# Expert results of a perceiver kernel collected rank by rank behind the row gathers, and spare rows filled in another stage

## The chip, the cores and the metric

The kernel runs on one core of one Trainium2 chip. The metric is the device time of one execution in microseconds (us), shown as the median of three timed runs. The core has TensorE (PE: matrix products; PEld is its weight load), VectorE (DVE), ScalarE (ACT), GpSimd (POOL) and SyncE (SP); sixteen DMA engines move data between HBM and the on-chip memories SBUF and PSUM. SP, ACT and POOL each issue DMAs on a queue of their own.

## The reference

Two layers of a perceiver in float32, on x of 16 x 64 tokens (1,024 tokens of 256 numbers) and a context of 16 x 1,601 rows of 256. Each layer adds three blocks to x, each on a layer-normalised x:

```
x += cross attention over ctx_1024 (masked)            # layer 0: "x0"
x += latent attention, 16 heads of 16, causal
x += position-routed feed-forward, 8 matrices
x += cross attention over ctx_1024                     # layer 1: "x1"
x += state-space mixer
x += mixture of experts:
      scores = sigmoid(x @ gate_w.T);  4 of 8 groups, then the 8 best of 64 experts
      w = scores of the 8 / their sum * 2.5
      y = sum over the 8 of  w * (silu(x @ Wg) * (x @ Wu)) @ Wd
      + a shared expert
```

The last block is the one that the larger part of the change touches: 8,192 (token, expert) pairs.

## The kernel before

**Cross attention x0.** Eight steps, one for each pair of batches. Step p needs two loads from HBM: ctxT(p), the context by columns (`load_columns`, L202, 3,202 KB), for the scores (L302), and ctxN(p), the same by rows (`load_rows`, L205 and L208, 3,202 KB together), for the products with the probabilities (L327). Both are double-buffered. SP issues ctxT(p+2) once scores(p) are done, and ctxN(p+1) once the products of step p-1 are done; all of it goes through SP's one queue, in program order. TensorE's order in a step is scores(p), products of p-1, transposes of p, and the output of p-1. After step 1's loads SP runs `x0_second` (L2195): the sixteen small weight loads of the latent attention (L129) and then eight DMAs (L2199) from HBM to HBM that fill y_rows from row 8,192 on with rows of x. These are the spare rows: tiles 64 to 127 of y_rows, which may be read without having been written in this execution. Then come ctxT(4), ctxN(3), ctxT(5) and so on. ACT waits for the fill (`s_spare`, L2078) before the expert tiles, over 600 us later. The latent attention's own SP block issues only one DMA, `WF.loads`, the 2 MB of feed-forward weights. Cross attention x1 is the same code with other weights; its `x1_second` issues the mixer's weights (about 3.3 MB) in the place of the fill.

**Experts: the routing.** DVE finds for each token its eight experts, and for each pair a slot, which is a row number in y_rows; `slots8` holds a token's eight slots in descending order (MAX8), so rank k = 7 is the smallest slot and k = 0 the largest. One-hot tiles (`of_tile`, `in_tile`, L1892, L1893) and products on TensorE (L1740, L1744) turn this into a list of tokens by slot (`idxt`, L1901).

**Experts: the tiles.** Slots are worked off in tiles of 128 rows, in rounds of six (RING = 6): 6 rounds of tiles that have their own weights, then 7 rounds in which two tiles' worth of weights serve three tiles; 78 tiles in all. For tile n POOL gathers 128 rows of x (L2086), TensorE turns and multiplies them (L1979, L1998, L2016), DVE copies and multiplies (L2037, L2045), ACT evaluates silu (L2062), copies the result (L2067) and stores it in y_rows (L2077). DVE hands POOL the index column of tile n + 5 in step n (L2029), and tile n's store is issued in step n + 7. After the last gather POOL waits until all rounds are stored.

**Experts: the collection.** A block of its own behind the tiles. For j = 0 to 7 (128 tokens each) and k = 0 to 7, POOL gathers the 128 rows of y_rows that hold the tokens' result of rank k (L2128, 64 indirect DMAs of 128 KB). Meanwhile DVE works out the weights (L2140 to L2159, 30 instructions), waits for the eight gathers of a j and adds them (L2171, 64 instructions), and ACT stores each j (L2135).

Of the kernel before, what the change touches and what calls it, by code (L numbers as in the profile page):

```python
# [40 lines left out]
def perceiver(nc, a, out):  # L41
    with ExitStack() as ctx:
        def sb(name, shape, dt=F32, own=ctx, side="left"):
            return own.enter_context(nc.sbuf_tensor(name, shape, dt, side=side))
        def sem(name, own=ctx):
            return own.enter_context(nc.semaphore(name))
# [687 lines left out]
        def latent_and_ffn(w, prep, x1, sem):  # L734
# [11 lines left out]
            def latent_attention():  # L746
# [882 lines left out]
        def experts(w):  # L1629
# [24 lines left out]
            w8 = own("w8", [P, NT, 8])  # L1654
            pick = own("pick", [P, NT, E])
            in_tile = own("in_tile", [P, 2, 4, P, 2], BF16)
            RING = 6
            LEAST, MOST = 2, 21
            LEAST2, MOST2 = 1, E // 4
# [39 lines left out]
            s_im = sem("moe_index_product")  # L1699
            with nc.Block(no_gpsimd_drain=True) as block:  # L1700
# [4 lines left out]
                def _(pe):  # L1705
# [79 lines left out]
                def _(dve):  # L1785
# [98 lines left out]
                    nc.vector.tensor_copy(place[:], sloti[:, 1:3, :, :])  # L1884
                    dve.drain()
                    for j in range(NT):
                        u = j % 2
# [5 lines left out]
                        nc.vector.tensor_tensor(in_tile[:, u], bc(count2[:], 1, 4), pairs_of(place[:, 1, j, :], P), ALU.is_equal).then_inc(s_oh, 1)  # L1893
                    dve.wait_ge(s_im, NT)
# [32 lines left out]
            s_ys = [sem(f"tile_stored{m}") for m in range(RING)]  # L1927
            GU, DOWN, AHEAD = 3, 6, 5
# [13 lines left out]
            def run(eng, step, lag):  # L1942
                for n in range(LEAST * RING):
                    step(n, n % RING, n // RING, None, lambda k, n=n: n >= k)
# [9 lines left out]
                with eng.Fori(LEAST, first) as g:  # L1954
                    whole(g)
# [16 lines left out]
            with nc.Block(no_gpsimd_drain=True) as block:  # L1972
# [54 lines left out]
                def _(dve):  # L2027
# [21 lines left out]
                    run(dve, step, GU)  # L2049
                @block.scalar  # L2050
                def _(act):
# [27 lines left out]
                    run(act, step, DOWN + 1)  # L2079
                @block.gpsimd  # L2080
                def _(pool):
                    def step(n, m, g, q, live):
# [5 lines left out]
                                                     ).then_inc(s_ga[m], 16)  # L2088
                    run(pool, step, 0)
                    rounds = whole_rounds(pool) + shared_rounds(pool)  # L2090
# [3 lines left out]
                def _(sp):  # L2094
# [12 lines left out]
                    for g in range(LEAST):  # L2107
# [3 lines left out]
                    with sp.Fori(LEAST, first) as g:  # L2111
                        whole(g)
# [4 lines left out]
            yg = own("yg", [P, NT, 8 * D])  # L2117
            s_yg = [sem(f"moe_collected{r}") for r in range(NT)]
            s_yl = [sem(f"moe_collected_last_{x}") for x in ("middle", "one")]
            s_ya = sem("moe_result_added")  # L2120
            def collected(j, k):
                return s_yg[j] if j < NT - 1 or k < 4 else s_yl[k // 7]
            with nc.Block(no_gpsimd_drain=True) as block:  # L2123
                @block.gpsimd
                def _(pool):
                    for j in range(NT):
                        for k in range(8):
                            nc.gpsimd.indirect_dma_start(out=yg[:, j, k * D:(k + 1) * D], out_offset=None, in_=y_rows[0:MOST_TILES * P, :],  # L2128
                                                         in_offset=bass.IndirectOffsetOnAxis(ap=sloti[:, 0, j, k:k + 1], axis=0)
                                                         ).then_inc(collected(j, k), 16)  # L2130
                @block.scalar
                def _(act):
                    for j in range(NT):
                        act.wait_ge(s_ya, j + 1)
                        act.dma_start(out.rearrange("(j b) s d -> j (b s) d", b=2)[j], xt[:, j, :]).then_inc(s_out, 16)  # L2135
                    act.wait_ge(s_out, 16 * NT)
                @block.vector
                def _(dve):
                    def choice_weights():
                        nc.vector.tensor_tensor(cwt[:], sg[:], rep[:], ALU.mult)  # L2140
                        dve.drain()
                        nc.vector.tensor_reduce(tot[:], cwt[:], AX, ALU.add)
                        dve.drain()
                        nc.vector.tensor_scalar(tot[:], tot[:], 1e-20, None, ALU.add)
                        dve.drain()
                        nc.vector.reciprocal(tot[:], tot[:])
                        dve.drain()
                        nc.vector.tensor_scalar(tot[:], tot[:], 2.5, None, ALU.mult)
                        dve.drain()
                        nc.vector.tensor_tensor(cwt[:], cwt[:], bc(tot[:], 2, E), ALU.mult)  # L2150
                        dve.drain()
                    def weight_third(i):
                        k, third = i // 3, i % 3
                        if third == 0:
# [7 lines left out]
                    for i in range(24):  # L2162
                        weight_third(i)
# [173 lines left out]
```

## Time and profile before

| | us |
|---|---|
| median of three runs | 927.86 |
| the three runs | 921.66, 927.86, 929.37 |
| the profiled execution | 924.3 |
| its span in the trace | 922.5 |

The page of the profile gives busy time by engine: PE 690.4 us (75% of the span), PEld 473.8, DVE 447.2, ACT 243.6, POOL 249.8. Its strip of 40 slices shows where the bound lies: PE is busy in nearly all of the first 36 slices, the DMA engines are full in the two cross attentions and in the expert tiles, and in the last four slices PE does nothing while POOL and DVE work. The mean granted clock of TensorE is 0.845 of full speed (2.4 GHz). A line of a timeline is: start, duration, engine, source line, operation, output and inputs, number of merged instructions, and in brackets the engine's idle time before it and what ended it. SPq and ACTq are DMA issues; the duration of a merged row reaches from the first to the last.

### The profile page before, as it was taken

What the parts mean: (1) busy time and instruction counts of PE and PEld (TensorE: products, weight loads), DVE (VectorE), ACT (ScalarE), POOL (GpSimd) and SP (SyncE); (2) the same over time, 40 slices, a digit from 0 to 9 for tenths busy, and PEclk for the clock granted to TensorE, in tenths of its full rate; (3) what the DMA queues carried; (4) which work ended last, traced back from release to release, by engine and by line L of the source; (5) the groups of instructions that cost most, each with busy time, mean ns of one, the idle gap of its engine ahead of it and who ended that gap; (6) DMA issues with size and microseconds to landing.
All of it is one profiled execution on the core that took longest, in us unless ns stands there. A gap on an engine that the chain in (4) does not pass through costs nothing. (4 is left out here: it accounts for less than half of the span.)

```text
span 922.5 us, 18970 instructions
## 1 busy us (share of the span) xinstructions
PE 690.4 (75%) x6637; PEld 473.8 (51%) x6637; DVE 447.2 (48%) x1114; ACT 243.6 (26%) x471; POOL 249.8 (27%) x289
## 2 busy tenths in 40 slices
PE   6798389896867699998899979796649899990000
PEld 4355155644645355555654468685448777770000
DVE  4333023357756452232436649858834334437534
ACT  1122021166445121211223644203412223330000
POOL 1011000020134120000000436512235445526775
PEclk9899699988968599999979965579779999995555
DMA  8999999420028969999117942001049999972343
GB/s 344 380 402 330 355 404 410 159 91 1 2 58 316 322 246 334 405 411 392 72 35 163 213 114 74 4 2 47 1 132 334 331 304 300 310 259 88 116 115 105
DMA packets 70888, 195.62 MB, mean 212 GB/s; under 512 B 11832, under 2 KB 43552, under 8 KB 65824
## 3 DMA queue, kind: packets, MB, share of 16 engines
q1 hardware_dynamic: 41248, 155.31, 47.6%
q10 hardware_dynamic: 22752, 20.72, 6.8%
q0 software_dynamic: 6816, 18.62, 6.8%
q8 instruction: 46, 0.75, 0.3%
q14 instruction: 26, 0.21, 0.1%
HBM read 181.05 MB, written 21.95 MB: 220 GB/s over the span
## 5 line engine op out<-in xcount | busy, mean ns | idle before, releaser
L2086 POOL DMA_INDIRECT moe_xg<-xn_rows,moe_idx x78 | 73.9, 948 | 83.4 <-DVE moe_idx L2029 72.3
L2128 POOL DMA_INDIRECT moe_yg<-y_rows,moe_sloti x64 | 64.0, 1000 | 37.2 <-issue 19.2
L302 PE MATMUL ps<-x0ctxT,x0qcur 128*64 128x512 f32 (+1 forms) x256 | 51.9, 562 | 22.8 <-DMA x0ctxT<-ctx_T 18.4
L1472 POOL TENSOR_TENSOR ss_dec<-ss_dec,ss_cT 128x256 f32<-128x256 f32 x48 | 39.7, 860 | 91.4 <-ACT ss_dec L1427 51.3
L2045 DVE TENSOR_TENSOR moe_hidT<-moe_silu,ps 128x128 f32<-128x128 f32 (+1 forms) x64 | 20.3, 317 | 80.5 <-ACT moe_silu L2062 59.6
L1285 PE MATMUL ps<-xnT,w_win 128*128 128x512 f32 x128 | 59.0, 620 | 0.0
L327 PE MATMUL ps<-x0ctxN,x0pT 128*64 128x256 f32 (+1 forms) x416 | 46.6, 381 | 7.4 <-issue 5.2
L327 PE MATMUL ps<-x1ctxN,x1pT 128*64 128x256 f32 (+1 forms) x416 | 46.6, 380 | 7.4 <-issue 5.2
L1317 PE MATMUL ps<-ss_dec 64*64 64x32 f32 (+2 forms) x1792 | 46.1, 256 | 6.1 <-issue 4.5
L91 POOL TENSOR_TENSOR rstd<-vare,neghalf 128x2 f32<-128x2 f32 (+1 forms) x10 | 11.2, 1125 | 139.5 <-DVE vare L87 139.5
L2062 ACT ACTIVATE moe_silu<-ps 128x128 f32<-128x128 f32 (+1 forms) x64 | 19.2, 300 | 109.0 <-issue 72.2
L302 PEld LDWEIGHTS ps<-x0ctxT,x0qcur 128*64 128x64 f32 x256 | 18.7, 150 | 57.1 <-issue 40.1
L302 PE MATMUL ps<-x1ctxT,x1qcur 128*64 128x512 f32 (+1 forms) x256 | 46.9, 520 | 1.0 <-POOL x1qcur L568 1.0
L2171 DVE SCALAR_TENSOR_TENSOR xt<-moe_yg,moe_w,xt 128x256 f32<-128x256 f32 x64 | 31.1, 486 | 33.8 <-DMA moe_yg<-y_rows,moe_sloti 29.1
L1317 PEld LDWEIGHTS ps<-ss_dec 64*64 64x64 f32 (+2 forms) x1792 | 39.7, 172 | 12.0 <-issue 7.1
L327 PEld LDWEIGHTS ps<-x0ctxN,x0pT 128*64 128x64 f32 (+1 forms) x416 | 32.2, 137 | 20.3 <-issue 9.3
L327 PEld LDWEIGHTS ps<-x1ctxN,x1pT 128*64 128x64 f32 (+1 forms) x416 | 32.3, 137 | 19.8 <-issue 9.0
L1998 PE MATMUL ps<-moe_xgT,e_shared_gate_up_weights 128*128 128x192 f32 x224 | 41.7, 330 | 0.1
L1285 PEld LDWEIGHTS ps<-xnT,w_win 128*128 128x128 f32 x128 | 25.1, 199 | 30.7 <-issue 30.3
L1979 PE MATMUL ps<-ident,moe_xg 128*128 128x128 f32 x156 | 32.4, 291 | 10.4 <-DMA moe_xg<-xn_rows,moe_idx 10.3
L1545 DVE COPY_PREDICATED ss_gm<-w_c_lvl,ps 128x128 f32<-128x128 int32 (+1 forms) x80 | 30.7, 384 | 18.6 <-ACT ss_gm L1441 13.1
L1998 PE MATMUL ps<-moe_xgT,moe_gate_up_weights 128*128 128x128 f32 x288 | 39.3, 281 | 0.0
(387 smaller groups left out, 1384.6 us busy)
## 6 DMA issues: line engine op xcount, KB each, us to landing
x0ctxT<-ctx_T SPq DMA_DIRECT2D x8, 3202.0 KB, 25.4
x1ctxT<-ctx_T SPq DMA_DIRECT2D x8, 3202.0 KB, 13.6
x0ctxN<-ctx SPq DMA_DIRECT2D x8, 3072.0 KB
x1ctxN<-ctx SPq DMA_DIRECT2D x8, 3072.0 KB
y_rows<-moe_ysb ACTq DMA_DIRECT2D x78, 128.0 KB
moe_gate_up_weights<-moe_gate_up SPq DMA_DIRECT2D x36, 256.0 KB, 4.5
e_shared_gate_up_weights<-moe_gate_up SPq DMA_DIRECT2D x28, 256.0 KB, 4.9
ss_dec<-seg_rows SPq DMA_DIRECT2D x8, 768.0 KB, 17.0
```

Source lines behind the costliest of these rows:

```text
L302: mm = pe.matmul(ps[64 * b:64 * b + 64, n, 0:k1 - k0], qcur[:, u, h, 64 * b:64 * b + 64], ctxT[:, u, b, h, k0:k1], start=h == 0, stop=h == ...
L327: mm = pe.matmul(ps[64 * b:64 * b + 64, 6, 0:D], pT[0:k, u, c, 64 * b:64 * b + 64], ctxN[0:k, u, b, c, :], start=c == 0, stop=c == NC_ - 1)
L1285: mm = pe.matmul(ps[:, 2 * slot[i] + n, :], win[:, h, m * P:(m + 1) * P], xnT[:, h, n * 512:(n + 1) * 512], start=h == 0, stop=h == DH - 1)
L1317: return pe.matmul(dst, f, g, start=True, stop=True)
L1472: e.tensor_tensor(f, f, g, ALU.mult).then_inc(s, 1)
L1545: ins = nc.vector.copy_predicated(old, bc(mask, 1, 4), new)
L1979: mm = pe.transpose(ps[:, TURNED[m % 3], h * P:(h + 1) * P], xg[:, m, h * P:(h + 1) * P], ident[:])
L1998: mm = pe.matmul(ps[:, PRODUCT[place % 3], x * w:(x + 1) * w], weights[:, h, x * FE:(x + 1) * FE], xgT[:, h, col:col + w], start=h == 0, s ...
L2045: nc.vector.tensor_tensor(hidT[:, col:col + w], silu[:, col:col + w], ps[:, PRODUCT[place % 3], w:2 * w], ALU.mult).then_inc(s_hh, tiles)
L2086: nc.gpsimd.indirect_dma_start(out=xg[:, m, :], out_offset=None, in_=xn_rows, in_offset=bass.IndirectOffsetOnAxis(ap=idx[:, m:m + 1], axis ...
L2128: nc.gpsimd.indirect_dma_start(out=yg[:, j, k * D:(k + 1) * D], out_offset=None, in_=y_rows[0:MOST_TILES * P, :], in_offset=bass.IndirectO ...
L2171: ins = nc.vector.scalar_tensor_tensor(xt[:, j, :], y[:, k, :], w8[:, j, k:k + 1], xt[:, j, :], ALU.mult, ALU.add)
```

## The change

- The eight fill DMAs of spare rows move from `x0_second` (SP, middle of cross attention x0) to the latent attention's SP block, behind `WF.loads`.
- The block of the collection is gone. POOL collects in the block of the tiles, directly behind its last row gather, and by rank: k = 7 first, k = 0 last, for each k all eight j. Ahead of a rank it loads a number of rounds from SBUF (`needed`), and waits until that many rounds are stored, with six waits on a register's value.
- The routing works out `needed`: for each rank the largest slot over all tokens, divided by 768, plus one. That is one reduction over j on DVE, a transpose on PE, a second reduction, a one-row product and five instructions on eight numbers.
- DVE works out the weights directly behind its last tile, in the same block, and adds by rank; for k = 0 it waits for each j alone. The 64 additions and 64 gathers are as many as before. The buffer `yg` (64 KB per partition) is now held beside the tiles' buffers.
- The written-out rounds stay two (WRITTEN); the least numbers of rounds rise from 2 and 1 to 3 and 2, which the data's 6 and 7 exceed.

```diff
@@ latent attention, sync
                         issue(sp, WF.loads)
+                        for r in range(SPARE):
+                            t0, t1 = T * 8 // P + r * NT, min(T * 8 // P + r * NT + NT, MOST_TILES)
+                            sp.dma_start(y_rows[t0 * P:t1 * P, :], a["x"].rearrange("b s d -> (b s) d")[0:(t1 - t0) * P, :]).then_inc(s_spare, 16)
@@ routing, tensor
+                    pe.wait_ge(s_lt, 1)
+                    pe.transpose(ps[0:8, 2, 0:P], latest[:], ident[:]).then_inc(s_lr, 1)
                     for j in range(NT):
+                        if j == 4:
+                            pe.wait_ge(s_lt, 2)
+                            pe.matmul(ps[0:1, 2, P:P + 8], latest_row[:, 0:1], ident[0:8, 0:8], start=True, stop=True).then_inc(s_lr, 1)
@@ routing, vector
+                    nc.vector.tensor_reduce(latest[:], slots8[:].rearrange("p j k -> p k j"), AX, ALU.max).then_inc(s_lt, 1)
                     dve.drain()
                     for j in range(NT):
+                        if j == 2:
+                            dve.wait_ge(s_lr, 1)
+                            nc.vector.tensor_reduce(latest_row[:], ps[0:8, 2, 0:P], AX, ALU.max).then_inc(s_lt, 1)
...
+                    dve.wait_ge(s_lr, 2)
+                    nc.vector.tensor_scalar(latest_int[:], ps[0:1, 2, P:P + 8], -1.0, None, ALU.add)
+                    dve.drain()
+                    nc.vector.tensor_scalar(latest_int[:], latest_int[:], 7, None, ALU.arith_shift_right)
+                    dve.drain()
+                    nc.vector.tensor_scalar(latest_int[:], latest_int[:], 171, None, ALU.mult)
+                    dve.drain()
+                    nc.vector.tensor_scalar(latest_int[:], latest_int[:], 10, None, ALU.arith_shift_right)
+                    dve.drain()
+                    nc.vector.tensor_scalar(needed[:], latest_int[:], 1, None, ALU.add)
                     dve.wait_ge(s_im, NT)
@@ tiles, vector
                     run(dve, step, GU)
...
+                    choice_weights()
+                    for i in range(24):
+                        weight_third(i)
+                    for k in reversed(range(8)):
+                        if k:
+                            dve.wait_ge(s_yg[k], 16 * NT)
+                        for j in range(NT):
+                            if k == 0:
+                                dve.wait_ge(s_yl[j], 16)
+                            ins = nc.vector.scalar_tensor_tensor(xt[:, j, :], yg[:, k, j, :], w8[:, j, k:k + 1], xt[:, j, :], ALU.mult, ALU.add)
+                            if k == 0:
+                                ins.then_inc(s_ya, 1)
+                        dve.drain()
@@ tiles, gpsimd
+                    def collect(k):
+                        rounds = pool.value_load(needed[0:1, k:k + 1], min_val=1, max_val=MOST + MOST2)
+                        stored = nc.gpsimd.to_reg(rounds * 16)
+                        pool.wait_ge(s_rows, 16)
+                        for m in range(RING):
+                            pool.wait_ge(s_ys[m], stored)
+                        for j in range(NT):
+                            nc.gpsimd.indirect_dma_start(out=yg[:, k, j, :], out_offset=None, in_=y_rows[0:MOST_TILES * P, :],
+                                                         in_offset=bass.IndirectOffsetOnAxis(ap=sloti[:, 0, j, k:k + 1], axis=0)
+                                                         ).then_inc(s_yg[k] if k else s_yl[j], 16)
                     run(pool, step, 0)
+                    for k in reversed(range(8)):
+                        collect(k)
                     rounds = whole_rounds(pool) + shared_rounds(pool)
@@ behind the tiles
-            with nc.Block(no_gpsimd_drain=True) as block:
-                @block.gpsimd
-                def _(pool):
-                    for j in range(NT):
-                        for k in range(8):
-                            nc.gpsimd.indirect_dma_start(out=yg[:, j, k * D:(k + 1) * D], out_offset=None, in_=y_rows[0:MOST_TILES * P, :],
...
@@ cross attention x0, sync
-        def x0_second(sp):
-            issue(sp, loads_la)
-            for r in range(SPARE):
-                t0, t1 = T * 8 // P + r * NT, min(T * 8 // P + r * NT + NT, MOST_TILES)
-                sp.dma_start(y_rows[t0 * P:t1 * P, :], a["x"].rearrange("b s d -> (b s) d")[0:(t1 - t0) * P, :]).then_inc(s_spare, 16)
-        cross_attention("x0", w_x0, True, bufs0, x0_first, x0_second, prep)
+        cross_attention("x0", w_x0, True, bufs0, x0_first, lambda sp: issue(sp, loads_la), prep)
```

## Rows read from the trace of the kernel before

**Rows 1.** The page: span, and the chain that ended last, by line.

```profile
span 922.5 us, 18970 instructions
...
POOL moe_yg L2128 7%; DMA moe_yg<-y_rows,moe_sloti 0%; DVE xt L2171 0%; DVEq L2172 0%; PEldq L2123 0%
```

**Rows 2.** Timeline of POOL, end of the tiles and the collection.

```profile
815.29 0.94 POOL L2086 DMA_INDIRECT moe_xg<-xn_rows,moe_idx  x1 [0.86 <-DVE moe_idx L2029]
834.25 0.94 POOL L2128 DMA_INDIRECT moe_yg<-y_rows,moe_sloti  x1 [18.02 <-PEq L2123]
...
916.46 0.95 POOL L2128 DMA_INDIRECT moe_yg<-y_rows,moe_sloti  x1 [0.31 <-issue]
```

**Rows 3.** Timeline of ACT: stores of tile 71 and of the last two tiles.

```profile
826.22 0.35 ACTq L2077 DMA_DIRECT2D y_rows<-moe_ysb  x1
...
829.75 1.92 ACTq L2077 DMA_DIRECT2D y_rows<-moe_ysb  x2
```

**Rows 4.** Timeline of DVE: last tile, first weight instruction, first additions.

```profile
827.88 0.35 DVE L2045 TENSOR_TENSOR moe_hidT<-moe_silu,ps 128x192 f32<-128x192 f32 x1 [1.25 <-ACT moe_silu L2062]
833.59 0.69 DVE L2140 TENSOR_TENSOR moe_cwt<-moe_sg,moe_rep 128x512 f32<-128x512 f32 x1 [5.36 <-PEq L1972]
...
855.46 5.02 DVE L2171 SCALAR_TENSOR_TENSOR xt<-moe_yg,moe_w,xt 128x256 f32<-128x256 f32 x9
```

**Rows 5.** Timeline of SP's queue in cross attention x0.

```profile
56.13 0.37 SPq L129 DMA_DIRECT2D w_wdq<-L_attn_W_DQ  x1
...
70.20 0.42 SPq L129 DMA_DIRECT2D w_kn<-L_attn_k_norm_w  x1
70.66 5.05 SPq L2199 DMA_DIRECT2D y_rows<-x  x8
76.11 0.41 SPq L202 DMA_DIRECT2D x0ctxT<-ctx_T  x1
```

**Rows 6.** DMAs of line L2199, from issue to landing.

```profile
DMA to landing us min/median/max: 6.1/14.7/23.5
```

**Rows 7.** Timeline of PE in x0: scores(3), (4), (7), products of steps 6 and 7.

```profile
75.59 5.60 PE L302 MATMUL ps<-x0ctxT,x0qcur 128*64 128x512 f32 x32
...
106.80 7.94 PE L302 MATMUL ps<-x0ctxT,x0qcur 128*64 128x512 f32 x32 [16.59 <-DMA x0ctxT<-ctx_T]
...
158.46 5.60 PE L302 MATMUL ps<-x0ctxT,x0qcur 128*64 128x512 f32 x32
165.83 5.83 PE L327 MATMUL ps<-x0ctxN,x0pT 128*64 128x256 f32 x52 [1.77 <-issue]
...
175.67 5.84 PE L327 MATMUL ps<-x0ctxN,x0pT 128*64 128x256 f32 x52 [0.60 <-DVE xt L436]
```

**Rows 8.** Stretches: PE, PEld, DVE, ACT, POOL busy (instructions); clock, DMA share, GB/s.

```profile
71.00:98.00 27.00, 18.88 (x134) 11.43 (x130) 7.09 (x15) 4.57 (x8) 0.62 (x2) 0.93 0.97 324
98.00:106.00 8.00, 0.00 (x0) 0.00 (x0) 0.00 (x0) 0.00 (x0) 0.00 (x0) 0.50 1.00 403
106.00:168.00 62.00, 53.92 (x361) 30.83 (x363) 18.24 (x56) 10.96 (x17) 0.80 (x2) 0.96 1.02 401
...
200.00:244.00 44.00, 33.39 (x445) 21.36 (x443) 31.29 (x50) 24.54 (x38) 2.17 (x3) 0.88 0.01 1
```

**Rows 9.** Timeline of PE in x1: scores(3), (4) and (5).

```profile
365.28 5.61 PE L302 MATMUL ps<-x1ctxT,x1qcur 128*64 128x512 f32 x32
...
379.92 5.60 PE L302 MATMUL ps<-x1ctxT,x1qcur 128*64 128x512 f32 x32
...
396.62 5.61 PE L302 MATMUL ps<-x1ctxT,x1qcur 128*64 128x512 f32 x32
```

**Rows 10.** Timeline of DVE: a small reduction, the wait behind the one-hots, a round's turn.

```profile
654.86 0.28 DVE L1867 TENSOR_REDUCE moe_owner<-moe_below 128x2 f32<-128x128 f32 x1
...
677.12 0.29 DVE L1896 COPY moe_home<-ps 128x128 f32<-128x128 f32 x1 [2.76 <-PE ps L1744]
...
705.63 0.15 DVE L2029 TENSOR_SCALAR moe_idx<-moe_idxt 128x1 int32 x1 [1.47 <-issue]
```

More of the change, by code:

```diff
@@ L1654, in experts @@
             w8 = own("w8", [P, NT, 8])
+            yg = own("yg", [P, 8, NT, D])
+            latest = own("latest", [P, 8])
+            latest_row = own("latest_of_choice", [8, 1])
+            latest_int = own("latest_int", [1, 8], I32)
+            needed = own("rounds_needed", [1, 8], I32)
             pick = own("pick", [P, NT, E])
@@ L1927, in experts @@
             s_ys = [sem(f"tile_stored{m}") for m in range(RING)]
+            s_yg = [None] + [sem(f"moe_choice_collected{k}") for k in range(1, 8)]
+            s_yl = [sem(f"moe_last_choice_collected{j}") for j in range(NT)]
+            s_ya = sem("moe_result_added")
             GU, DOWN, AHEAD = 3, 6, 5
@@ L1942, in run @@
             def run(eng, step, lag):
-                for n in range(LEAST * RING):
+                for n in range(WRITTEN * RING):
                     step(n, n % RING, n // RING, None, lambda k, n=n: n >= k)
@@ L1953, in shared @@
                         step(g * RING + m, m, g, q, lambda k: True)
-                with eng.Fori(LEAST, first) as g:
+                with eng.Fori(WRITTEN, first) as g:
                     whole(g)
@@ L2079, in _ @@
                     run(act, step, DOWN + 1)
+                    for j in range(NT):
+                        act.wait_ge(s_ya, j + 1)
+                        act.dma_start(out.rearrange("(j b) s d -> j (b s) d", b=2)[j], xt[:, j, :]).then_inc(s_out, 16)
+                    act.wait_ge(s_out, 16 * NT)
                 @block.gpsimd
@@ L2106, in shared @@
                             load(0 if g is None else g * RING + m, etab[0:1, 1, ds(q * 4 + x, 1)], wgu2[:, x], s_wl2[x])
-                    for g in range(LEAST):
+                    for g in range(WRITTEN):
                         whole(g)
@@ L2110, in _ @@
                     second = shared_rounds(sp)
-                    with sp.Fori(LEAST, first) as g:
+                    with sp.Fori(WRITTEN, first) as g:
                         whole(g)
@@ L2116, in experts @@
             rings.close()
[L2117 to L2122, printed above, removed]
-            with nc.Block(no_gpsimd_drain=True) as block:
-                @block.gpsimd
-                def _(pool):
-                    for j in range(NT):
-                        for k in range(8):
-                            nc.gpsimd.indirect_dma_start(out=yg[:, j, k * D:(k + 1) * D], out_offset=None, in_=y_rows[0:MOST_TILES * P, :],
[L2129 to L2154, printed above, removed]
-                            nc.vector.tensor_tensor(pick[:], slot1[:], bc(slots8[:, :, k], 2, E), ALU.is_equal)
-                        elif third == 1:
-                            nc.vector.tensor_tensor(pick[:], pick[:], cwt[:], ALU.mult)
-                        else:
-                            nc.vector.tensor_reduce(w8[:, :, k], pick[:], AX, ALU.add)
-                        dve.drain()
-                    choice_weights()
-                    for i in range(24):
-                        weight_third(i)
-                    for j in range(NT):
-                        y = yg[:, j, :].rearrange("p (k d) -> p k d", k=8)
-                        for k in range(8):
-                            if k == 0:
-                                dve.wait_ge(s_yg[j], 16 * (8 if j < NT - 1 else 4))
-                            if j == NT - 1 and k in (4, 7):
-                                dve.wait_ge(s_yl[k // 7], 16 * (3 if k == 4 else 1))
-                            ins = nc.vector.scalar_tensor_tensor(xt[:, j, :], y[:, k, :], w8[:, j, k:k + 1], xt[:, j, :], ALU.mult, ALU.add)
-                            dve.drain()
-                        ins.then_inc(s_ya, 1)
```

30 lines of the change are left out of this document (28 added, 2 removed).

## The prediction

> **What bounds the kernel now.** I read the page first. The chain that ended last is POOL's own: the 64 gathers of the collection and nothing else [rows 1]. The timeline of POOL shows why: the last row gather starts at 815.29, then POOL idles 18.02 us for the end of the tiles' block, and the 64 gathers run from 834.25 to 916.46, one each (916.46 - 834.25)/63 = 1.305 us [rows 2]. In these 82 us PE is idle and DVE keeps up. So the end of the kernel is POOL's time: what starts the 64 gathers earlier shortens the kernel one for one. ACT's timeline places the last stores: tile 71 at 826.22, tiles 76 and 77 at about 829.75 and 831.3 [rows 3].
>
> The second place is cross attention x0, which the page's strip shows with full DMAs. The timeline of SP's queue has the small latent weights from 56.13, the eight fill DMAs at 70.66, and only behind them ctxT(4) at 76.11 [rows 5]. The timeline of PE has scores(3) at 75.59 and scores(4) at 106.80, after 16.59 us of waiting for ctxT(4), and then taking 7.94 us instead of 5.60 [rows 7]. So the fill is on the path of x0, not beside it.
>
> **Part 1: the fill leaves x0.** The fill writes tiles 64 to 127, 64 x 128 KB = 8.39 MB. Its last landing is 23.5 us after an issue at about 75.1, so at 98.6 [rows 5, 6]: 28 us of the DMA engines, which move 324 GB/s from 71 to 98 [rows 8]. Behind it nine context loads of 3.28 MB wait in one queue: ctxT(4), ctxN(3), ctxT(5), ctxN(4), ctxT(6), ctxN(5), ctxT(7), ctxN(6), ctxN(7). At the 401 GB/s of the stretch 106 to 168 [rows 8] each takes 8.2 us, together 73.6: 98.6 + 73.6 = 172.2, and the products of step 7 start at 175.67 [rows 7]. Without the fill the same chain starts at 71.5 (SP is free at 70.6, the small latent loads are still in the engines [rows 5]) and ends at 71.5 + 73.6 = 145.1.
>
> PE has a pace of its own. In x1, where the mixer's 3.3 MB stand in the place of the fill, scores(3) and (4) start at 365.28 and 379.92, 14.64 us apart, with no wait [rows 9]. Then x0 would have scores(4) at 75.59 + 14.6 = 90.2 instead of 106.80, and scores(7) at 90.2 + 3 x 14.6 = 134.0. From scores(7) to the products of step 7 it is 17.21 us, of which 1.77 are waiting [rows 7], so 15.4: 149.4. I checked each load against its use: ctxT(4) lands at 80 (used at 90.2), ctxN(3) 88 (95.6), ctxT(5) 96 (104.8), ctxN(4) 104 (110.2), ctxN(5) 120 (124.8), ctxN(6) 137 (139.4), ctxN(7) 145 (149.4). The margin at ctxN(6) is 2.5 us, thin but there. The step gains 175.67 - 149.4 = **26.2 us**. The lower bound is x1's course: there scores(5) follows scores(4) after 16.70 [rows 9], a pace that the loads set. If x0 fell into that too, only scores(4)'s wait goes: 31.21 - 14.64 = 16.6, and 18.73 - 16.70 = 2.0 for the clock (scores(5) start at 106.80 + 18.73 in the trace), 18.6 in all. I take 26.2, because the x0 chain would start 4.1 us ahead of scores(3), while x1's loads wait behind the mixer's weights.
>
> The clock, told by rows: PE's granted clock is 0.93 from 71 to 98, with PE busy for 18.9 of 27 us, and 0.50 (1.2 GHz) from 98 to 106, where PE does nothing [rows 8]; scores(4) start at that lower level, hence their 7.94 us [rows 7]. That goes with the stall and is inside the 26.2.
>
> **Where the fill goes.** The latent attention starts its block near 190.8 - 26; the fill then lies under it for some 28 us behind 2 MB of weights, 37 us together. From 200 to 244 the DMAs move 1 GB/s [rows 8], and the next loads on this queue come at about 270 - 26. ACT's wait for the fill is 500 us later. So it costs nothing; if fetches of instructions, which pass through the same engines (a queue of their own on the page), got stuck behind it, I allow 2 us in the range.
>
> **Part 2: the collection moves up.** Which rounds a rank needs depends on data, so I worked the slots out from the reference's own routing on its inputs: 36 own tiles and 28 shared sets, 6 and 7 rounds, as many weight loads as the trace has. The rounds needed are 7, 10, 10, 12, 12, 13, 13, 13 for k = 7 to 0. POOL could start at 815.29 + 0.94 + 0.30 = 816.5 instead of 834.25: **-17.7 us** [rows 2]. Do the waits cost? Ranks 7, 6 and 5 need round 10, tile 59, whose store is issued before 807. Rank 4 needs round 12, tile 71, issued at 826.22 [rows 3] and landed by about 830; POOL arrives there after 24 gathers, at 816.5 + 24 x 1.305 = 847.8. Rank 2 needs round 13, landed by 834; POOL arrives at 868.7. No wait is ever open, with 17 us to spare, so later stores are covered too.
>
> New on POOL is, per rank, a load of a number from SBUF, a multiplication and seven waits. Before has no such thing between two gathers. The nearest row is DVE's turn from the written-out rounds to the loop, 1.47 us with two such loads [rows 10], so at most 0.7 per load; the lower bound is 0, since the row gathers have two waits and register work ahead of each and still the 0.30 us gap of gathers without any. I take 0.5 each, 8 x 0.5 = **+4.0**, bounds 0 to 8. The Trainium skill, "DMA: Bandwidth & Descriptors", Latency and other measured facts, gives a load of this kind a floor of about 600 ns. By it the term would be an estimated 4.8.
>
> DVE: the weights start behind its last tile, at 828.2 instead of 833.59, and take as long as before, 855.46 - 833.59 = 21.9 [rows 4], to 850.1. By then POOL has 25 gathers out; the additions go at 5.02/9 = 0.56 us [rows 4] against POOL's 1.305, so the backlog is gone by about 865, 30 us before the end. Behind the last gather lie one addition and one store, as before. The gathers from 816 to 831 share the DMAs with the last stores; a tile delayed by a few us hits nobody, as the waits have 17 us.
>
> **Part 3: the routing.** The first reduction (128x64, like 0.28 us [rows 10]) stands ahead of the one-hots on DVE's path: +0.3. The second, the transpose and the small product fall into waits for ACT. The five small instructions, some 0.25 us each with their drains, 1.25, lie in DVE's 2.76 us wait for PE [rows 10]. Without that cover they would cost the 1.25. I take **+0.4**.
>
> **Sum.** 924.3 - 26.2 - 17.7 + 4.0 + 0.4 = 884.8 for an execution like the profiled one. The median of the runs is 3.6 above it; 884.8 + 3.6 = 888.4, so **888 us**.
>
> **Rivals.**
> *x0 goes by its loads.* Gain of part 1 is 18.6 rather than 26.2, time 896. For it: x1's pace of 16.70 and the thin margin at ctxN(6). Against it: the margins above. A rule leads to the same place: at a lower rate the nine loads are late. At 358 GB/s each is 9.2 us, the chain ends at 71.5 + 82.5 = 154, the gain is some 21 and the time 893. The Trainium skill, "DMA: Bandwidth & Descriptors", Where 436 GB/s comes from, puts the limit of HBM loads at about 358 GB/s per core. By that rule this rival would be the forecast; the trace disagrees, with 401 GB/s over 62 us.
> *The collection gains nothing.* If POOL in fact sits until the last store (its waits or its index column tie it to the end), the time is 924.3 - 26.2 + 0.4 + 3.6 = 902. The rounds worked out speak against it.
> *x0 gains nothing*: something else, SP's small loads say, holds ctxT(4). Then 884.8 + 26.2 + 3.6 = 915. Against it: from 71 to 98.6 the queue holds the fill ahead of ctxT(4).
> *The other side: the fill slows the latent attention.* Its 37 us of full DMAs would have to hold up fetches of instructions by more than 26.2 + 17.7 - 4.4 = 39.5 us before the kernel gets no faster, and by 49 for 1% slower. x0 itself ran at PE's full pace under full DMAs, so I hold it to be unlikely.
>
> **How the numbers follow.** Forecast 0.66, x0 by its loads 0.20, collection without gain 0.05, x0 without gain 0.04, fill in the way 0.05 (of it 0.02 slower, 0.01 same, 0.02 still faster). Low end: no load costs and no offset to the median, 888.4 - 4.0 - 3.6 = 881, and 1 or 2 less in x0: 879. High end: the first rival, 896, with 2 us more for loads on POOL: 898. Of the first two cases nearly all lies inside, some 0.8 in all. A measurement of this kernel can tell about 1% from no change (the three runs span 0.8%). Faster by over 1% (under 918.6): 0.66 + 0.20 + 0.05 + 0.04 + 0.02 = 0.97, of which I move 0.01 to same for what I have not seen: 0.96, 0.02, 0.02.
>
> **What the profile after would show.** PE's scores(4) near 90 without a wait for ctxT, scores 14.6 apart and products of step 7 near 149; if they are 16.4 apart, the first rival. A DMA strip with full slices in the latent attention, none of its engines slower. POOL's 64 gathers behind the last row gather, the first within 1.5 us of its end, with no gap above 1 us. A gap of several us ahead of rank 4 or 2 would prove the rounds wrong. DVE's additions waiting for POOL from about the 40th on. The prediction fails if a gap per rank is above 1 us or if the load chain sags below 380 GB/s.

## The result

Medians over several executions, each kernel beside runs of the kernel before on the same chip. One execution of e5 below, at 888.20 us, is over 1.5% slower than the fastest of its kernel and is left out of its median and range.

| | before | after |
|---|---|---|
| median, us | 924.76 | 886.5 |
| lowest and highest, us | 914.96 to 929.37 | 880.23 to 889.74 |
| ratio after/before, 95% interval | | 0.9612 [0.9501, 0.9723] |
| the profiled execution, us | 924.3 | 880.23 |
| its span, us | 922.5 | 878.3 |
| its mean granted clock | 0.845 | 0.86 |

The forecast was 888 us. The kernel became 3.9% faster, and the median is 1.5 us from the forecast. The two spans differ by 44.2 us, where the terms of the sum add up to 39.5. They are followed in order of time.

**Cross attention x0.** The timeline of SP's queue in the kernel after answers to [rows 5], with the fill in its new place behind the weight w_wf (start, duration, engine and line):

```profile
70.51 0.42 SPq L129 DMA_DIRECT2D w_kn<-L_attn_k_norm_w  x1
71.33 0.40 SPq L202 DMA_DIRECT2D x0ctxT<-ctx_T  x1
...
166.36 0.38 SPq L129 DMA_DIRECT2D w_wf<-L_ffn_WT  x1
166.78 6.38 SPq L780 DMA_DIRECT2D y_rows<-x  x8
...
238.18 0.38 SPq L129 DMA_DIRECT2D w_x_wq<-L_xattn_Wq  x1
```

ctxT(4) is issued at 71.33 instead of 76.11. The timeline of PE answers to [rows 7]: scores(3), (4), (5) and (7), then the products of steps 6 and 7.

```profile
75.03 5.61 PE L302 MATMUL ps<-x0ctxT,x0qcur 128*64 128x512 f32 x32
...
89.59 5.60 PE L302 MATMUL ps<-x0ctxT,x0qcur 128*64 128x512 f32 x32
...
104.14 5.61 PE L302 MATMUL ps<-x0ctxT,x0qcur 128*64 128x512 f32 x32
...
133.93 5.60 PE L302 MATMUL ps<-x0ctxT,x0qcur 128*64 128x512 f32 x32
141.35 5.83 PE L327 MATMUL ps<-x0ctxN,x0pT 128*64 128x256 f32 x52 [1.82 <-issue]
...
151.19 5.83 PE L327 MATMUL ps<-x0ctxN,x0pT 128*64 128x256 f32 x52 [0.60 <-DVE xt L436]
```

Nothing waits ahead of scores(4), and scores follow each other after 14.6 us up to the sixth; the seventh comes 15.2 us later, since the products of step 5 waited 0.46 us. The products of step 7 start 175.67 - 151.19 = 24.5 us earlier. The windows answer to [rows 8]: the full clock (1.00, 2.4 GHz) where PE had stood still at 0.50, and one stretch in the latent attention that now has DMA work under it. The first row is the start of the chain of context loads.

```profile
71.00:73.00 2.00, 1.91 (x16) 1.26 (x12) 0.70 (x3) 0.56 (x1) 0.00 (x0) 1.00 0.48 61
71.00:98.00 27.00, 26.66 (x190) 15.15 (x188) 9.23 (x18) 4.79 (x9) 0.80 (x2) 1.00 0.97 380
98.00:106.00 8.00, 7.83 (x55) 4.94 (x53) 2.47 (x6) 2.93 (x5) 0.00 (x0) 1.00 1.01 404
...
166.30:238.20 71.90, 52.70 (x760) 36.27 (x761) 53.55 (x100) 42.04 (x69) 12.47 (x13) 0.94 0.43 147
```

The loads ctxT(4) and ctxT(7), from issue (71.33 and 109.94) to landing:

```profile
DMA to landing us min/median/max: 12.0/12.0/12.0
...
DMA to landing us min/median/max: 22.2/22.2/22.2
```

So ctxT(4) landed at 83.3 and ctxT(7) at 132.1. The same view gives 99.5 for ctxT(5) and 115.7 for ctxT(6).

The latent attention of the kernel before, from the issue of w_wf to that of x1's first weight, in its windows:

```profile
190.80:269.90 79.10, 60.09 (x760) 40.13 (x760) 53.54 (x100) 42.50 (x69) 12.46 (x13) 0.83 0.09 28
```

The same 760 matmuls, DVE busy for as long to 0.01 us, and yet 7.2 us less, at a granted clock of 0.94 instead of 0.83. No step of the prediction had this.

**Routing.** From DVE's MAX8 to the first row gather it takes 22.46 us instead of 21.67, 0.8 more. In DVE's timeline the five new small instructions lie ahead of the copy that waited for PE in [rows 10]; it still waits, 1.76 instead of 2.76:

```profile
643.72 0.14 DVE L1915 TENSOR_SCALAR moe_latest_int<-ps 1x8 int32<-1x8 f32 x1
644.64 0.16 DVE L1923 TENSOR_SCALAR moe_rounds_needed<-moe_latest_int 1x8 int32<-1x8 int32 x1
646.56 0.29 DVE L1926 COPY moe_home<-ps 128x128 f32<-128x128 f32 x1 [1.76 <-PE ps L1760]
```

**The collection.** The timeline of POOL answers to [rows 2]. The rank of the first eight gathers is k = 7, the one at 796.75 is the first of k = 6.

```profile
785.18 0.95 POOL L2158 DMA_INDIRECT moe_xg<-xn_rows,moe_idx  x1 [0.70 <-DVE moe_idx L2062]
786.73 0.95 POOL L2168 DMA_INDIRECT moe_yg<-y_rows,moe_sloti  x1 [0.60 <-DMA y_rows<-moe_ysb]
787.98 0.95 POOL L2168 DMA_INDIRECT moe_yg<-y_rows,moe_sloti  x1 [0.30 <-issue]
...
796.75 0.95 POOL L2168 DMA_INDIRECT moe_yg<-y_rows,moe_sloti  x1 [0.30 <-issue]
...
842.68 1.12 POOL L2168 DMA_INDIRECT moe_yg<-y_rows,moe_sloti  x1 [0.30 <-issue]
844.10 1.67 POOL L2168 DMA_INDIRECT moe_yg<-y_rows,moe_sloti  x1 [0.30 <-issue]
846.08 0.95 POOL L2168 DMA_INDIRECT moe_yg<-y_rows,moe_sloti  x1 [0.30 <-issue]
...
871.77 0.97 POOL L2168 DMA_INDIRECT moe_yg<-y_rows,moe_sloti  x1 [0.30 <-issue]
```

The first gather starts 1.55 us behind the start of the last row gather, instead of 18.96. Between ranks the gap is the usual 0.30 us. But the pace is (871.77 - 786.73)/63 = 1.350 us where before had 1.305, and the reason stands in the second column: some gathers take 1.12 or 1.67 us instead of 0.95. DVE's timeline at that time (compare [rows 4]):

```profile
820.09 9.91 DVE L2114 SCALAR_TENSOR_TENSOR xt<-moe_yg,moe_w,xt 128x256 f32<-128x256 f32 x24
...
841.70 3.26 DVE L2114 SCALAR_TENSOR_TENSOR xt<-moe_yg,moe_w,xt 128x256 f32<-128x256 f32 x8 [7.74 <-DMA moe_yg<-y_rows,moe_sloti]
852.64 3.25 DVE L2114 SCALAR_TENSOR_TENSOR xt<-moe_yg,moe_w,xt 128x256 f32<-128x256 f32 x8 [7.68 <-DMA moe_yg<-y_rows,moe_sloti]
```

The eight additions of a rank run one behind another from 841.70 to 844.96, and the two long gathers lie under them. The kernel before drained DVE behind each addition, that is, let it end before the next was issued; the change drains once per rank.

The account, from the two profiles:

| stretch | before | after | difference | forecast |
|---|---|---|---|---|
| start to the products of x0's step 7 | 175.67 | 151.19 | -24.5 | -26.2 |
| latent attention, w_wf to x_wq | 79.07 | 71.82 | -7.2 | 0 |
| routing, MAX8 to first row gather | 21.67 | 22.46 | +0.8 | +0.4 |
| last row gather's end to the end | 106.27 | 92.17 | -14.1 | -17.7 + 4.0 |

The other stages add up to +0.8: the feed-forward stretch up to x1's first scores -0.7, x1 with the mixer 0.0, the routing's head +1.1, the tiles +0.4. All together: -44.2. Within the last row, -17.4 is the earlier start (18.96 to 1.55), +2.8 the slower pace, and +0.5 lies behind the start of the last gather.

### The profile page after: what moved, and what is told of

Read it like the earlier page. It is cut to its first block and busy times, and to the rows that moved or that the text cites. A ratio compares the mean times of both kernels' runs of the same rounds, so it can differ in the third digit from the quotient of the medians.

```text
span 878.3 us, 18973 instructions
## 1 busy us (share of the span) xinstructions
PE 683.1 (78%) x6640; PEld 472.3 (54%) x6640; DVE 443.2 (50%) x1121; ACT 243.8 (28%) x471; POOL 253.5 (29%) x289
## 5 line engine op out<-in xcount | busy, mean ns | idle before, releaser
L2168 POOL DMA_INDIRECT moe_yg<-y_rows,moe_sloti x64 | 66.8, 1044 | 19.8 <-issue 18.3
L302 PE MATMUL ps<-x0ctxT,x0qcur 128*64 128x512 f32 (+1 forms) x256 | 46.5, 516 | 6.6 <-issue 5.8
L2114 DVE SCALAR_TENSOR_TENSOR xt<-moe_yg,moe_w,xt 128x256 f32<-128x256 f32 x64 | 26.5, 480 | 29.6 <-DMA moe_yg<-y_rows,moe_sloti 29.3
```

The lines of the kernel that those rows point to most:

```text
L302: mm = pe.matmul(ps[64 * b:64 * b + 64, n, 0:k1 - k0], qcur[:, u, h, 64 * b:64 * b + 64], ctxT[:, u, b, h, k0:k1], start=h == 0, stop=h == ...
L2114: ins = nc.vector.scalar_tensor_tensor(xt[:, j, :], yg[:, k, j, :], w8[:, j, k:k + 1], xt[:, j, :], ALU.mult, ALU.add)
L2168: nc.gpsimd.indirect_dma_start(out=yg[:, k, j, :], out_offset=None, in_=y_rows[0:MOST_TILES * P, :], in_offset=bass.IndirectOffsetOnAxis(a ...
```

## The experiments

Each number with brackets behind it is the ratio to the kernel before, with its 95% interval; a range in parentheses is the lowest and highest execution. e3, e8, e10 and e11 fill 16 spare tiles instead of 64; the other spare rows stay unwritten, which the data of this case never read. All the others compute everything. The measure for the collection is the time from the last row gather's end to the end of the span, "the tail stretch": 106.27 us before, 92.17 after.

**Two halves.** e1 is the kernel before with only the fill moved; e2 is the changed kernel with the fill back in x0.

```diff
 e1:                     issue(sp, WF.loads)
+                        for r in range(SPARE):
+                            ... sp.dma_start(y_rows[...], ...).then_inc(s_spare, 16)
...
 x0_second:
-            for r in range(SPARE):
-                ... sp.dma_start(y_rows[...], ...).then_inc(s_spare, 16)
```

> The kernel before with only the eight fill DMAs moved to the latent attention. Theory: the move is worth the 24.5 us by which the products of step 7 came earlier in the changed kernel (175.67 to 151.19), so a time of 0.973 to 0.975 of before, and the products of step 7 at 150 to 152. Rival 1 (the fill only changes its place): the latent attention gives part of it back, ratio above 0.985. Rival 2 (x0 goes by its loads): step 7 at about 157, ratio 0.98.

> The changed kernel with the fill put back into cross attention x0, so that only the collection and the routing differ from before. Theory: from the end of the last row gather to the end of the span 93 us instead of before's 106.3, ratio 0.985 to 0.988 of before (11 to 14 us). Rival: the gathers start early but the tiles' own last rounds are slowed and the end moves by less than 5 us, ratio above 0.995.

e1: 895.24 us (893.53 to 901.73), 0.9681 [0.9612, 0.9751], against 926.84 before. Products of step 7 start at 151.18, as in the changed kernel; the tail stretch is 105.21. e2: 909.65 us (905.91 to 914.94), 0.982 [0.9747, 0.9892]. Products at 176.57, tail stretch 91.0, 2 us less than the 93 expected. Its POOL timeline:

```profile
816.36 0.95 POOL L2155 DMA_INDIRECT moe_xg<-xn_rows,moe_idx  x1 [0.87 <-DVE moe_idx L2059]
817.91 0.95 POOL L2165 DMA_INDIRECT moe_yg<-y_rows,moe_sloti  x1 [0.60 <-DMA y_rows<-moe_ysb]
```

By the medians the fill is worth 31.6 us and the collection 17.2. Together that is 48.8, where the change brought 38.3 in its own measurement and 38.8 in that of e0 below. In the traces the parts do add up: x0 gives 24.5 in e1, which is just what it gives after, and the tail stretch 15.3 in e2 and 14.1 after. What e1 has beyond its 24.5 lies in part in the latent attention, 74.45 us instead of 79.07, where no engine's instructions differ and only the fill's DMAs are new; that is taken up below.

**Is it the rounds that free the collection?** e4 lets every rank wait for all 13 rounds:

```diff
-                        rounds = pool.value_load(needed[0:1, k:k + 1], min_val=1, max_val=MOST + MOST2)
+                        rounds = whole_rounds(pool) + shared_rounds(pool)
                         stored = nc.gpsimd.to_reg(rounds * 16)
```

> The changed kernel, but every rank waits until all 13 rounds are stored, as if the rounds by rank were not known. Theory: the first gather of results then starts when the last store has landed, 17 us behind the last row gather instead of 0.6, and the whole of it reaches the end: 16 to 17 us slower than the changed kernel, near 0.98 of before. Rival: the gain came from the missing block boundary and not from the early start; then it is within 4 us of the changed kernel.

902.18 us (898.05 to 905.3), 0.9723 [0.9655, 0.979]. Its POOL timeline:

```profile
793.61 0.95 POOL L2158 DMA_INDIRECT moe_xg<-xn_rows,moe_idx  x1 [1.01 <-DVE moe_idx L2062]
811.66 0.95 POOL L2168 DMA_INDIRECT moe_yg<-y_rows,moe_sloti  x1 [17.11 <-DMA y_rows<-moe_ysb]
```

The 18 us are back, and the tail stretch is 108.14. By the medians it is 16 us slower than the changed kernel's 886.5 (18 than e0's 884.35), as expected. The last row gather's start and the first gather of results are 18.05 us apart here, 18.96 before. But e1 and e8, which keep the block of its own, have 18.01 and 18.03, so that the collection stands in the tiles' block is worth nothing that the traces show: 0.9 us against one profile, none against two. The gain comes from ranks that ask for early rounds. This is also the prediction's rival "the collection gains nothing", built as a kernel: it was priced at 902.

**What do the number and the seven waits per rank cost?** e6 has the rounds of this data as constants, so neither load nor multiplication:

```diff
-                        rounds = pool.value_load(needed[0:1, k:k + 1], min_val=1, max_val=MOST + MOST2)
-                        stored = nc.gpsimd.to_reg(rounds * 16)
+                        stored = (13, 13, 13, 12, 12, 10, 10, 7)[k] * 16
```

> The changed kernel with the rounds by rank written in as constants (7, 10, 10, 12, 12, 13, 13, 13), so no load and no multiplication per rank on POOL, the waits stay. Theory: the load is hidden behind the gather ahead of it (the gap between ranks is 0.30 us, that within a rank too), so pace and time are those of the changed kernel, the first gap perhaps 0.3 shorter. Rival, the prediction's term: 0.5 us a rank, 4 us less.

e0 is the changed kernel again, beside it on the same chip:

> The changed kernel once more, unchanged, to stand beside the others of this row on the same chip, and for a second profile. Expected: 0.955 to 0.965 of before; collection and cross attention x0 within 0.5 us of the first profile; the latent attention anywhere from 72 to 80 us, with the granted clock from 0.94 to 0.82 to match.

e6: 880.21 us (875.11 to 882.06), 0.9521 [0.9473, 0.957]. e0: 884.35 us (880.59 to 887.37), 0.9572 [0.9521, 0.9623]. The intervals overlap, so the trace must tell. In e6 the first gather follows the last row gather by 1.25 us instead of 1.55, the pace is 1.332 against e0's 1.323, and the tail stretch 90.45 against 90.15. The load costs 0.3 us once and nothing at the other seven ranks.

e0 also shows how far one profile can be trusted. Its x0 and its routing are those of the first profile (products of step 7 at 151.30, routing 22.46), but its pace is 1.323 instead of 1.350 and its tail stretch 90.15 instead of 92.17. That is 2.0 us, where at most 0.5 was expected. The same kernel thus gained 14.1 us in the tail stretch in one execution and 16.1 in the other.

**What makes the gathers slower?** e5 puts the drain back behind each addition; e9 leaves the additions as they are and starts them only when the last gather is in.

```diff
 e5:                         ins = nc.vector.scalar_tensor_tensor(xt[:, j, :], yg[:, k, j, :], ...)
-                        dve.drain()
+                            dve.drain()
 e9:                         weight_third(i)
+                    dve.wait_ge(s_yl[NT - 1], 16)
                     for k in reversed(range(8)):
```

> The changed kernel with a drain behind each of the 64 additions, as before had them, instead of one behind each eight. In the changed kernel the 64 gathers go at 1.350 us each, before at 1.305, and gathers of 1.67 us lie beside DVE's runs of eight undrained additions. Theory: the runs of additions slow POOL; with drains the pace is 1.30 to 1.31 and the end 2 to 3 us earlier than in the changed kernel, none of the gathers behind rank 4 above 1.3 us. Rival 1: the pace comes from the order by rank; it stays at 1.34 to 1.35. Rival 2: it comes from the loads and waits per rank; the same.

> The changed kernel, but DVE starts its 64 additions only when the last gather has landed, so that none of them lies beside a gather; the weights still do. Theory: every gather behind the weights' end (from about the 28th on) takes 0.94 to 0.96 us with a gap of 0.30, a pace of 1.25, and the whole 64 average 1.28 or less; the end comes later by the additions' 26 us less what they overlapped. Rival: some other agent slows POOL; then gathers of 1.1 us and more stay.

e5: 880.59 us (874.88 to 882.24), 0.9535 [0.9491, 0.958]; pace 1.299, tail stretch 89.07. POOL and DVE at the place where the changed kernel has 1.12 and 1.67:

```profile
842.74 0.95 POOL L2168 DMA_INDIRECT moe_yg<-y_rows,moe_sloti  x1 [0.30 <-issue]
843.99 0.95 POOL L2168 DMA_INDIRECT moe_yg<-y_rows,moe_sloti  x1 [0.30 <-issue]
...
841.81 4.45 DVE L2114 SCALAR_TENSOR_TENSOR xt<-moe_yg,moe_w,xt 128x256 f32<-128x256 f32 x8 [3.52 <-DMA moe_yg<-y_rows,moe_sloti]
```

e9, in a single execution (901.84 us, since the additions now stand behind everything):

```profile
842.67 0.94 POOL L2169 DMA_INDIRECT moe_yg<-y_rows,moe_sloti  x1 [0.30 <-issue]
...
870.41 26.56 DVE L2115 SCALAR_TENSOR_TENSOR xt<-moe_yg,moe_w,xt 128x256 f32<-128x256 f32 x64 [50.60 <-DMA moe_yg<-y_rows,moe_sloti]
```

With DVE idle, every gather from the 26th on takes 0.94 or 0.95 us, and the pace over all is 1.278, since gathers under the weights still reach 1.34 (1.47 in e3). So the work of DVE lengthens POOL's gathers, and dense additions do it more: over 64 gathers POOL is busy for

```profile
L2168 POOL DMA_INDIRECT moe_yg<-y_rows,moe_sloti x64 | 66.8, 1044 | 19.8 <-issue 18.3
```

in the changed kernel (line, engine, operation, count, busy and mean ns, idle), and in e5 for

```profile
L2168 POOL DMA_INDIRECT moe_yg<-y_rows,moe_sloti x64 | 63.8, 997 | 19.8 <-issue 18.3 <-DMA y_rows<-moe_ysb 1.5
```

with the same 19.8 of gaps. The size differs between executions: e0 has no gather above 1.28 us beside the additions and 65.2 us in all. But the five undrained profiles whose ranks start early have a pace of 1.323 to 1.350, the four drained ones (e5, e10, e11, e12) 1.297 to 1.307, and the kernel before, drained too, 1.305.

The Trainium skill, "SBUF — State Buffer", Who interferes with whom, says that a DVE instruction with two inputs in SBUF contends with a GpSimd instruction that reads SBUF. The additions have two such inputs (moe_yg and xt), and the gather reads its indices from SBUF; the traces agree with it, at 1.12 to 1.67 us against 0.95. The same section of the Trainium skill infers that such an instruction does not hold up GpSimd's writing of DMA descriptors; if that is part of the gather's time, these traces speak against it. Which of the gather's accesses collides was not separated.

**Does the drained kernel win as a whole?** e12 is e5 again, e10 is e5 with a quarter of the fill, e3 is the changed kernel with it:

```diff
-                        for r in range(SPARE):
+                        for r in range(2):
...
-                    act.wait_ge(s_spare, SPARE * 16)
+                    act.wait_ge(s_spare, 2 * 16)
...
-    in_=y_rows[0:MOST_TILES * P, :]
+    in_=y_rows[0:80 * P, :]
```

> The changed kernel with a drain behind each addition once more, as the partner of the kernel with the quarter fill, on one chip. Theory A and B both: latent attention 72 to 76; 0.950 to 0.957 of before; pace of the gathers 1.30.

> The drained kernel with the fill of 16 tiles instead of 64 in the latent attention. In ten profiles so far the latent attention took 71.8 to 76.1 us in the six with the full fill under it and 78.0 to 79.8 in the four with a quarter or none, always with the granted clock to match. Theory A (chance, the clock falls or not as its pauses happen to lie): lengths mixed, this one anywhere from 72 to 80, and no difference of medians against the drained kernel of the same row. Theory B (the fill's traffic goes with a higher clock): this one at 78 to 80 again, and its median 3 to 4 us above the drained kernel's.

> The changed kernel with a fill of 16 tiles instead of 64 (2.1 MB instead of 8.4 MB, two DMAs), still in the latent attention; spare rows beyond tile 80 are neither filled nor open to the gathers, which this data never needs. Theory: the latent attention hides the fill wholly, so no difference from the changed kernel within noise, and its engines' instructions take the same time. Rival: full DMA engines cost the latent attention something (fetches of instructions, ports); then this is 2 us or more faster and the stage from the feed-forward weights' issue to x1's first weights' issue is shorter than 71.8 us by that.

e12: 880.58 us (878.08 to 886.69), 0.9525 [0.9483, 0.9566]. e10: 881.38 us (879.91 to 882.92), 0.9537 [0.9504, 0.957]. e3: 887.29 us (886.71 to 889.46), 0.9581 [0.9524, 0.9639]. Tail stretches 88.69, 89.79 and 90.71. The stage gains: 88.7 to 89.8 in the four profiles with the drains, 90.2 to 92.2 in the five without (the changed kernel, e0, e2, e3, e6). For the whole kernel e5 and e12 both lie at 880.6 against 884.4 and 886.5, but the intervals overlap; for the whole kernel a gain of the stage's size, 0.4 to 3.5 us, is likely and not settled.

**Is the fill free in its new place, and whence the 7.2 us?** Two theories. A: the latent attention goes with the clock that it is granted, and this differs from run to run. B: the fill's traffic has to do with it. e3 spoke for B, with 79.80 us at 0.82 and a quarter of the fill, so e12 (full) and e10, e11 (quarter) were made. e11 is e10 again, in a single execution:

> The same kernel as the drained one with the quarter fill, for one more profile of its latent attention. Theory A: anywhere from 72 to 80 us. Theory B: 78 to 80.

879.61 us. The windows of the stage in e3, e11 and e12, in this order:

```profile
166.70:246.50 79.80, 60.84 (x761) 40.70 (x762) 53.58 (x100) 42.60 (x69) 12.42 (x13) 0.82 0.15 54
```

```profile
166.70:239.00 72.30, 53.07 (x761) 36.69 (x762) 53.58 (x100) 41.98 (x69) 12.48 (x13) 0.93 0.16 59
```

```profile
166.80:244.90 78.10, 59.04 (x760) 40.26 (x761) 53.56 (x100) 42.45 (x69) 12.42 (x13) 0.84 0.39 136
```

72.3 us with a quarter of the fill, 78.1 with all of it: as a rule for each execution B falls. The 78.1 also misses the 72 to 76 that both theories gave e12. e10 and e11 are one program and took 79.6 and 72.3, so most of the spread is A's. Over the profiles the length goes with the clock alone: 71.8 at 0.94, 72.3 at 0.93, 74.4 to 74.5 at 0.89, 75.8 to 76.1 at 0.87, 78.0 to 78.4 at 0.85, 78.1 at 0.84, 79.1 to 79.6 at 0.83, 79.8 at 0.82. That gives some 8 us to every single execution that no edit here makes. It also warns against reading e1 and e2 to a few us.

A weaker B stays open. The eight profiles with the whole fill under the stage average 75.2 us (71.8 to 78.1), the three with a quarter 77.2, and the three with none (before, e2, e8) 78.5 (78.0 to 79.1). The fill's traffic may go with a somewhat higher clock on average; fourteen single profiles don't settle it. What they do show is that the fill doesn't lengthen the stage. The medians agree: e10 and e12, with a quarter and all of the fill, have 881.38 and 880.58, though their intervals would hide 3 us either way.

**A smaller fill in x0.** e8 is the kernel before with 16 tiles filled where the 64 were, so that only the size of what stands ahead of ctxT(4) changes.

> The kernel before with a fill of 16 tiles instead of 64 (2.1 MB, two DMAs), left in cross attention x0; spare rows beyond tile 80 are neither filled nor open to the gathers. The chain of context loads then starts about 7 us later than without a fill, instead of 27. Theory: the loads have 10 us to spare at ctxT(4) but only 2.5 at ctxN(6), so scores(4) do not wait, and the products of step 7 come 4 to 5 us later than the 151.2 of the changed kernel, at 155 to 156. Rival: the cost goes by the megabyte (24.5/4 = 6 us from the start, with a wait at scores(4)); or the stall was not the fill's bytes but its place in SP's queue, then step 7 stays beyond 170.

904.1 us (901.06 to 907.0), 0.9803 [0.9753, 0.9853]. PE's timeline, scores(4), products of step 3, scores(5), products of step 4, and the products of step 7:

```profile
90.56 5.60 PE L302 MATMUL ps<-x0ctxT,x0qcur 128*64 128x512 f32 x32
97.30 5.83 PE L327 MATMUL ps<-x0ctxN,x0pT 128*64 128x256 f32 x52 [1.14 <-issue]
106.47 5.61 PE L302 MATMUL ps<-x0ctxT,x0qcur 128*64 128x512 f32 x32
113.35 5.83 PE L327 MATMUL ps<-x0ctxN,x0pT 128*64 128x256 f32 x52 [1.26 <-DMA x0ctxN<-ctx]
...
155.62 5.83 PE L327 MATMUL ps<-x0ctxN,x0pT 128*64 128x256 f32 x52 [0.60 <-DVE xt L436]
```

With the queue some 5 us later, x0 does go by its loads: scores stand about 16 us apart, and every product waits 1.1 to 1.5 us. The products of step 7 came as expected, at 155.62; the 16 us between scores were not. So the first rival is real and begins a few us away; without any fill the kernel is just on the other side of it.

## Why the prediction held, step by step

**x0, -26.2.** The mechanism held: the fill was ahead of ctxT(4), scores(4) came at 89.59 (forecast 90.2), scores(7) at 133.93 (forecast 134.0). The term was mis-sized by 1.7 us, at the place that it called thin: the products of step 6 waited 1.82 us, about the 1.77 of before that the sum had taken out. The step that was off is the start of the load chain. The sum let it run at 401 GB/s from 71.5, which puts ctxT(4) at 80; it landed at 83.3, 3.3 us late. The engines moved only 61 GB/s from 71 to 73, which is some 1.7 us of it; the rest stays open. From there the pace was the forecast's: ctxT(4) to (7) landed 16.2, 16.2 and 16.4 us apart, two loads each, and the last, at 132.1, was 3.2 us behind the 71.5 + 7 x 8.2 = 128.9 of the sum. One more load of 8.2 us puts ctxN(6) at an estimated 140.3 instead of 137, beyond the margin of 2.5. The trace marks the wait as issue and names no load, so this cause is argued; in the kernel before and in e8 one wait of the same kind names ctxN. The chain's rate was 380 GB/s from 71 to 98, the very bound at which the prediction said that it would fail, and 404 from 98 to 106. Luck is in it too: scores(3) began 0.56 us before the time taken from the kernel before, which made up for the 0.46 us that step 5 waited. The rival "x0 goes by its loads" (18.6) did not come, but it was 3 us nearer than the margins said.

**The fill in the latent attention, 0.** Right. The last of its eight DMAs, issued at 172.6, landed 27.6 us later, at 200.2, inside the stage's quiet stretch, and e10, e11 and e12 show no cost.

**The collection, -17.7.** Right: -17.4 against the profile before, -16.5 against e1 and e8, whose wait is 18.0. e4 shows that the ranks' early rounds make it. No rank waited for its round; the gap is 0.30 us everywhere but at the first, as the rounds worked out from the routing said.

**Loads on POOL, +4.0.** The sum was near in the first profile by luck, and its reason was false. The loads cost 0.3 us in all (e6), not 0.5 each: the step had no row for a load on POOL and took DVE's turn, which showed 1.47 us of idle time. It seems that POOL does its register work while a gather runs; the rows show only that the gap stays at 0.30. What did cost stood nowhere, 2.8 us in the first profile and 1.1 in e0: the change took the drains from between DVE's additions, the additions of a rank became a dense run of 3.26 us instead of 4.45 (e5), and the gathers under them went from 0.95 to as much as 1.67. DVE therefore waited for POOL ahead of its 25th and 33rd addition, and not from about the 40th. The prediction said that DVE's additions keep up and stopped there; it didn't ask what they do to POOL.

**Routing, +0.4.** 0.8, and the five instructions lie in DVE's wait for PE, as said: 1.76 us of it were left. Over all profiles the stretch takes 22.1 to 22.6 us with the new routing and 21.7 to 21.9 without it, so neither 0.4 nor 0.8 is exact.

**From the profiles to the median.** Without the latent attention's -7.2, for which the runs show no cause in the change beyond the open one named above, the account is -24.5 + 0.8 - 14.1 + 0.8 = -37.0 us. The medians differ by 38.3 us, and in e0's measurement by 38.8; the sum of the forecast's terms was -39.5. So the forecast gain was about 1 us too high by the medians and 2.5 by the traces. It was taken off a median of 927.9, and the kernel before was then measured at 924.76 and 923.17; hence 886.5 and 884.35 instead of 888. That the median came within 1.5 us is thus partly luck: the base was 3.1 us too high (927.86 against 924.76) and the gain 1.2 us too high, and the two offset. The changed kernel's profiled execution, 6 us below its median, is the one with the clock of 0.94 in the latent attention.

## To carry over

When a fill or a spill that nobody awaits stands ahead of loads in one queue, price the whole chain of loads behind it up to its last use, and move it under a stage with idle DMAs. When a barrier is split by what each piece truly needs, the gain is the barrier's wait, one for one, while later work on the same engine stays covered. When the bound engine gathers by indirect DMA, look at what VectorE does at its side: keep the drains between its two-input instructions, as e5 did. Spreading them in another way was not tried here.

## What the runs showed of the hardware

- An indirect gather of 128 rows on GpSimd takes 0.94 to 0.95 us and 0.30 of gap with VectorE idle; beside undrained additions from SBUF up to 1.28 in some executions and 1.68 in others, beside drained ones no more than 1.21 (e10), beside the weights' 128x512 instructions up to 1.47 (e3).
- A number loaded from SBUF, a multiplication and seven waits between two gathers cost GpSimd nothing that the rows show, behind a running gather.
- 8.39 MB written from one place of HBM to another in eight DMAs took from first issue to last landing 98.6 - 70.7 = 27.9 us in x0 and 200.2 - 166.8 = 33.4 us in the latent attention, where 2 MB of weights stood ahead. No DMA in these traces has PSUM at either end, other than the first section says; they go between HBM and SBUF or within HBM.
- One stage with the same matmuls took 71.8 to 79.8 us over fourteen profiles, at granted clocks of 0.94 to 0.82. Two executions of one program took 79.6 and 72.3 (e10, e11), two of another 71.8 and 75.8 (the changed kernel, e0).
